# Two of the eight softmax blocks of each head normalised on ScalarE in place of GpSimd

## What is computed

```
q, k, v = x.w_aq, x.w_ak, x.w_av       (per head)
q, k    = rope(q), rope(k)
s       = q.k^T / 128, entries with key > query masked
p       = softmax(s)                   (over the keys)
r       = (p.v).w_ao, summed over the heads
x       = layernorm(x + r);  x = layernorm(x + ffn(x))
ffn(x)  = w3(gelu(h2(gelu(h1(silu(w1(x)) * w2(x))))))
```

## Time and profile before

| what | value |
|---|---|
| median of 3 runs | 1065.4 us (1064.43 to 1065.68) |
| the profiled execution | 1065.99 us, of which 1064.2 us are the span of the profile |
| attention | from the start to about 768 us |
| feed-forward network | from about 790 us to the end |
| TensorE busy | 997.1 us, 94% of the span |
| VectorE, ScalarE, GpSimd busy | 820.6, 593.3 and 539.6 us |
| normalising (L703) | 256 instructions, 191.1 us |
| exponentials (L522) | 256 blocks, 190.5 us without the reading of sums |

### The profile page before, as it was taken

One profiled execution on the slowest core, in us unless ns is written; L12 is line 12 of the kernel. 1 busy time (PEld: TensorE's weight loads), 2 busy tenths in 40 slices (PEclk: granted clock), 3 DMA queues, 4 the chain that ended last, 5 costly groups with the idle time before them and its releaser, 6 DMA issues. The chain is left out here.

```text
span 1064.2 us, 19686 instructions
## 1 busy us (share of the span) xinstructions
PE 997.1 (94%) x5648; PEld 860.2 (81%) x5648; DVE 820.6 (77%) x1803; ACT 593.3 (56%) x1255; POOL 539.6 (51%) x536
## 2 busy tenths in 40 slices
PE   3799999999999999999999999999839999999995
PEld 3688888898888889888888888888728878788784
DVE  5888888888888888887888888788555677486744
ACT  3566666665666666566666666666434252433521
POOL 4666767776676776677677666767250101000000
PEclk9899999999999999999999999999969999999998
DMA  8433233432322123323222222221020000000000
GB/s 282 150 127 74 61 80 97 124 99 56 75 69 69 49 59 100 70 61 79 59 49 59 61 70 68 72 59 40 1 80 1 1 1 21 1 20 0 1 20 21
DMA packets 33292, 66.16 MB, mean 62 GB/s; under 512 B 5457, under 2 KB 6993, under 8 KB 32209
## 3 DMA queue, kind: packets, MB, share of 16 engines
q1 hardware_dynamic: 30400, 58.62, 21.0%
q10 hardware_dynamic: 2832, 6.82, 1.7%
HBM read 24.26 MB, written 7.34 MB: 30 GB/s over the span
## 5 line engine op out<-in xcount | busy, mean ns | idle before, releaser
L703 POOL TENSOR_SCALAR probs<-probs,inv_sum 128x128 f32<-128x128 f32 (+7 forms) x256 | 191.1, 747 | 232.4 <-DVE inv_sum L621 231.8
L534 ACT ACTIVATE pT<-psum 128x512 fp32r<-128x512 f32 (+3 forms) x384 | 173.9, 490 | 144.0 <-PE psum L401 141.9
L308 PE MATMUL psum<-pT,vals 128*128 128x512 f32 (+3 forms) x1152 | 242.6, 351 | 1.6 <-DVE rT L663 1.6
L522 ACT ACTIVATE probs<-psum,neg_max 128x128 f32<-128x128 f32 (+7 forms) x256 | 190.5, 744 | 80.2 <-DVE neg_max L615 79.8
L615 DVE TENSOR_REDUCE neg_max<-psum 128x1 f32<-128x128 f32 (+7 forms) x256 | 191.2, 747 | 54.8 <-PE psum L392 53.6
L631 DVE TENSOR_TENSOR pT<-psum,pT 128x512 fp32r<-128x512 f32 (+3 forms) x384 | 200.7, 551 | 32.3 <-ACT pT L534 25.3
L308 PEld LDWEIGHTS psum<-pT,vals 128*128 128x128 f32 x1152 | 187.7, 189 | 23.9 <-DVE pT L631 1.7
L401 PE MATMUL psum<-ident,probs 128*128 128x128 f32 x1152 | 173.7, 277 | 12.9 <-POOL probs L703 12.2
L883 PE MATMUL ps<-hid,w 128*128 128x512 f32 x768 | 181.3, 396 | 0.0
L708 POOL TENSOR_TENSOR swapped<-by_cos,swapped 128x512 f32<-128x512 f32 x128 | 164.7, 1298 | 14.2 <-DMA swapped<-by_sin 14.2
L883 PEld LDWEIGHTS ps<-hid,w 128*128 128x128 f32 x768 | 143.7, 188 | 34.5
(11 more groups left out here) (77 smaller groups left out, 1195.3 us busy)
## 6 DMA issues: line engine op xcount, KB each, us to landing
swapped<-by_sin SPq DMA_DIRECT2D x256, 128.0 KB, 2.3
w_stage<-qk_split SPq DMA_DIRECT2D x30, 256.0 KB, 2.7
wv_stage<-v_split SPq DMA_DIRECT2D x15, 256.0 KB, 2.7
x_split<-ffn_raw ACTq DMA_DIRECT2D x2, 1024.0 KB, 5.8
ffn_raw<-g SPq DMA_DIRECT2D x2, 1024.0 KB, 8.0
x_moving<-x_split SPq DMA_DIRECT2D x2, 1024.0 KB, 5.1
out<-y SPq DMA_DIRECT2D x4, 512.0 KB, 2.6
raw_x<-xT SPq DMA_DIRECT2D x3, 512.0 KB, 11.6
```

Of the source, the lines that this page charges most:

```text
L308: ins = nc.tensor.matmul(out_ap, left[a], right[b], start=first and i == 0, stop=last and i == 2)
L522: nc.scalar.activation(probs[:, ib % 4, :width].rearrange("p (h c) -> p h c", h=halves), score_ps[:, ib % 2, :halves, :half], ACT.Exp, bia ...
L534: nc.scalar.activation(pT[chunk][:, 0, 4 * f:4 * f + n_blocks, (ib % 4) * P:(ib % 4 + 1) * P], bank("t", head[1], nth)[:, :n_blocks * P].r ...
L703: nc.gpsimd.tensor_scalar(p, p, inv_sum[:, n:n + 1], 1.0, ALU.mult, ALU.mult).then_inc(probs_ready[0], 1)
```

## The change

ScalarE gets a function `scale_probs`: a Copy activation over the block in place, with the reciprocals of the rows as its scale (one number for each partition). It does this for blocks 3 and 5 of each head, as the last thing in its steps 2 and 4. GpSimd leaves these two out and keeps the other six. TensorE, ahead of its transposes, waits for GpSimd's semaphore or for the new one of ScalarE, by the block.

```diff
+ACT_SCALED = (3, 5)
+POOL_SCALED = tuple(i for i in range(8) if i not in ACT_SCALED)
...
-    probs_ready = (sem("probs_ready"), NI)
+    probs_scaled = (sem("probs_scaled"), len(POOL_SCALED))
+    probs_scaled_act = (sem("probs_scaled_act"), len(ACT_SCALED))
...
             def transpose_probs(head, ib):
-                wait_for(pe, probs_ready, head, ib)
+                if ib in ACT_SCALED:
+                    wait_for(pe, probs_scaled_act, head, ACT_SCALED.index(ib))
+                else:
+                    wait_for(pe, probs_scaled, head, POOL_SCALED.index(ib))
...
+            def scale_probs(head, ib):
+                n = parity(head) * NI + ib
+                p = probs[:, ib % 4, :(ib + 1) * P]
+                wait_for(act, inv_ready, head, ib)
+                nc.scalar.activation(p, p, ACT.Copy, scale=inv_sum[:, n:n + 1]).then_inc(probs_scaled_act[0], 1)
...
                 for c in v_tasks(head, s):
                     values_high(head[0], c)
+                if exists(ahead) and (s + 1) % NI in ACT_SCALED:
+                    scale_probs(ahead, (s + 1) % NI)
...
-                if exists(ahead):
+                if exists(ahead) and (s + 1) % NI in POOL_SCALED:
                     normalize(ahead, (s + 1) % NI)
```

More of the change, by code:

```diff
@@ L702, in normalize @@
                 p = probs[:, ib % 4, :(ib + 1) * P]
-                nc.gpsimd.tensor_scalar(p, p, inv_sum[:, n:n + 1], 1.0, ALU.mult, ALU.mult).then_inc(probs_ready[0], 1)
+                nc.gpsimd.tensor_scalar(p, p, inv_sum[:, n:n + 1], 1.0, ALU.mult, ALU.mult).then_inc(probs_scaled[0], 1)
             def rope_sum(head, j):
```

## The result

| | before | after |
|---|---|---|
| median | 1065.32 us (4 runs) | 1087.43 us (1087.17 to 1087.81, 4 runs) |
| the profiled execution | 1065.99 us | 1087.19 us |
| its span | 1064.2 us | 1085.4 us |

The ratio is 1.0209, with a 95% interval of 1.0191 to 1.0227: 22.1 us slower. The forecast was 1088 us, which is 22.7 us above this median before; the prediction's own sum was 22.4.

What follows compares the result with a forecast made beforehand. TensorE, nearly always busy in attention, was taken as the bound, held at block 6 in every head. 32 heads x 0.70 = 22.4 us added to a 1066.0 us profiled execution, less 0.6 to the median, gave 1088 us; range 1081 to 1096.

Steps and rivals of the forecast that it cites:

- The bound: TensorE's transposes of block 6 wait for GpSimd's normalising in every head, without slack; 0.65 us shown in head 17.
- The push: Block 5's copy on ScalarE delays the exponential of block 6 by 0.80 us, of which 0.70 reach TensorE.
- VectorE's cover: Between row sums and reciprocal of block 6, VectorE's earlier work hides the first 0.10 us of the delay.
- The two waits: TensorE waits 0.27 us for block 5's copy, inside its longer wait at block 6; a head still loses 0.70.
- The forecast's sign: In the profile after, transposes of block 5 wait for ScalarE, 0.2 to 0.3 us in each head.
- Block 3: Its copy on ScalarE delays the exponential of block 4 by 0.30 us, inside existing idle time; costs nothing.
- The cover: Block 3's delay fits in ScalarE's 0.55 us wait for GpSimd's rotary sum; its copy ends 2.6 us before TensorE asks.
- GpSimd's relief: Taking 64 of 256 multiplications off GpSimd brings block 6 no earlier, since it waits for the reciprocal; worth nothing.
- Waits that add up: Rival: each head pays the waits at blocks 5 and 6 both, 0.97 us, giving 1096 us; chance 11%.
- ScalarE as the bound: Rival: ScalarE's lag lasts into the next head, so block 7 pays too, 45 us, giving 1110 us; chance 4%.
- Slack in TensorE: Rival: TensorE's busy time is elastic and catches up behind each wait, giving about 1066 us; chance 6%.
- GpSimd as the bound: Rival: GpSimd holds back block 6, so relieving it makes the kernel faster, about 1055 us; chance 4%.

Runs made afterwards that it cites:

- block 5 alone: Against the kernel before, ScalarE normalises only block 5, at the change's place, and GpSimd the other seven: 1087.82 us, ratio 1.0217.
- its own run: Against the kernel before, ScalarE normalises only block 3 and GpSimd the other seven: 1065.18 us, ratio 0.9999.
- the early copies: The change with both ScalarE copies moved ahead of the split of the transposed block: 1065.56 us, ratio 1.0004 to the kernel before.
- the idle copies: Kernel before plus an unread ScalarE copy at the place of the change's block 5 copy: 1084.33 us with 768 columns, 1071.24 us with 256.
- the run with block 5 left out: Against the kernel before, no engine normalises block 5 and TensorE waits for its reciprocal instead: 1064.55 us, ratio 0.9992.

## Why the prediction was right

*The bound.* Right for a delay: block 6 has no slack in any head, even where no idle time was shown. The evidence was the same 0.06 us between GpSimd's end and TensorE's start. It was too narrow as a description: block 6 is one point of a chain of maximum, exponential, reciprocal and normalising through blocks 6 and 7, and from there VectorE's list leads into blocks 0 to 2 of the next head. A delay at block 6 delays everything; an advance at block 6 ends at block 7, and one at both blocks ends at VectorE. The prediction needed the first alone.

*The push.* Forecast 0.80 us from start to start, measured 0.83 (0.826 to 0.830 in the 32 heads). The estimate of 0.827 that the prediction worked out from the Trainium skill's "ScalarE: Activation LUTs", "What ACT_TABLE_LOAD costs", was the closer one. VectorE's cover was forecast at 0.10 and is 0.12 to 0.13. Both were too low by 0.02 to 0.03 and cancel, which is luck, worth 1 us of the sum: 0.70 forecast, 0.71 for block 5 alone. The duration of 0.92 us was 0.933.

*The two waits.* Right: transposes of block 5 are 0.29 us late in head 17 (1.64 us after the split of block 4, where it was 1.35), and the forecast was 0.27. In the even heads it is 0.18 to 0.26. This lies inside the wait for block 6. The forecast's sign, a wait for ScalarE in each head, is there by name in 10 heads only. In the other 22 the transposes start 0.13 us behind the copy's end in place of 0.05, and the profile names another releaser; no run shows what these 0.08 us are.

*Block 3.* Right, and shown by its own run. In head 17 after:

```profile
441.30 0.71 ACT L557 ACTIVATE probs<-probs,inv_sum 128x512 f32<-128x512 f32 x1
...
441.92 0.78 ACT L528 ACTIVATE probs<-psum,neg_max 128x640 f32<-128x640 f32 x1
...
442.68 1.15 ACT L550 ACTIVATE qk<-swapped 128x512 fp32r<-128x512 f32 x2
...
444.64 0.60 PE L407 MATMUL psum<-ident,probs 128*128 128x128 f32 x4
```

The cover held: the rotary copies of ScalarE now follow without waiting, where they had waited 0.55 and more, and the copy ended 2.6 us ahead of TensorE (1.3 us in the first and the last head).

*GpSimd's relief.* Worth nothing in 31 heads, as forecast. The forecast said 32. In the first head GpSimd and not the reciprocal came last, and after the change its transposes of block 6 came 0.41 us earlier behind those of block 5, where all other heads lost. So the sum has 31 terms of 0.71 us and this small gain in place of 32 equal terms, which is about 1 us less. That a group of 32 with 31.6 us of idle time holds one without any could have been seen in a timeline of the first head.

*The rivals.* Waits that add up (1096) and ScalarE as the bound (1110) are refuted by the time and by the early copies. Slack in TensorE (1066) is refuted by the idle copies: 0.18 us in each head is passed on in full, so the 77 us in which no weights were loaded were no slack for a push at block 6. GpSimd as the bound (1055) is refuted by the run with block 5 left out.

What stays open: that VectorE's list holds TensorE at blocks 0 to 2 is read from the traces; no run shortened that list to show what it would give.

## What to carry to other kernels

Ask of an added instruction not how busy its engine is, but what stands behind it in the engine's list and who waits for that: the same 0.93 us copy cost 0.71 us in one place and nothing two or three instructions earlier, on an engine that was idle for a third of the time. Price it by the distance from start to start, less what the next engine in the chain was late by anyway. Before shortening a wait, follow the chain past it to the next block: here 0.32 us gained at one block was waited for at the next, and 0.34 us gained over two blocks was waited for at VectorE.

## What the runs showed of the hardware

A copy on ScalarE with a scale read from memory takes about 0.09 us longer than one without: 933 ns and 843, both of 768 columns from SBUF to SBUF. The first is in place and the second is not, and no run tells the two apart; but two copies that are not in place differ by the same 92 ns, so being in place seems to cost nothing.

A row without idle time on TensorE does not mean that it was not held. In the even heads no gap was shown ahead of block 6, only the same 0.055 us from GpSimd's end to the transposes as in the odd heads. The idle copy of 256 columns, which came to 0.31 us less 0.13 of cover, still moved the transposes of these heads by 0.19.
